# Linear attention: one scan per unit, one GpSimd chain for the scales, high parts of gated values on ScalarE a unit later

## The reference, cut to what matters

```python
q = layernorm(silu(causal_dwconv(h @ Wq)))         # 4 taps; the same for k
v, beta, gate = h @ Wv, sigmoid(h @ Wb + bb), silu(h @ Wg)
def step(S, inp):                                  # over the tokens
    S = (1.0 - b) * S + b * (v_t[..., :, None] * k_t[..., None, :])
    return S, einsum('bhvk,bhk->bhv', S, q_t)
out = (o * gate) @ Wo
```

## Time and profile before

| | |
|---|---|
| device time, three runs | 1381.65, 1390.52, 1396.57 us; median 1390.52 |
| profiled execution | span 1388.4 us from first to last instruction; its own time is not listed apart from the span |
| busy share of the span | PE 90%, DVE 75%, ACT 51%, POOL 48% |
| mean granted TensorE clock | 0.958 of full speed |
| linear attention | first convolution tap 410.0 us, last addition to `x_tok` 1329.2 us |

### The profile page before, as it was taken

One profiled execution on the slowest core, in us unless ns is written; L12 is line 12 of the kernel. 1 busy time (PEld: TensorE's weight loads), 2 busy tenths in 40 slices (PEclk: granted clock), 3 DMA queues, 4 the chain that ended last, 5 costly groups with the idle time before them and its releaser, 6 DMA issues. The chain is left out here.

```text
span 1388.4 us, 23212 instructions
## 1 busy us (share of the span) xinstructions
PE 1247.3 (90%) x7062; PEld 959.6 (69%) x7062; DVE 1036.7 (75%) x2130; ACT 711.5 (51%) x1336; POOL 670.5 (48%) x1678
## 2 busy tenths in 40 slices
PE   4899999996978889998999998998999999899769
PEld 3455545445747778777877787877877787788646
DVE  6747676746337888888888888888888788788652
ACT  2236555572436464655555555646555555546323
POOL 6000000001606766666666766666666766676620
PEclk9569999998999999999999999999999999999989
DMA  6414333303020111001001101011000100010010
GB/s 150 52 31 56 54 48 47 47 2 105 2 80 25 35 54 35 24 24 64 32 25 54 34 23 65 23 34 54 34 23 23 64 29 28 24 34 12 1 61 1
DMA packets 25098, 56.00 MB, mean 40 GB/s; under 512 B 3831, under 2 KB 8823, under 8 KB 23863
## 3 DMA queue, kind: packets, MB, share of 16 engines
q1 hardware_dynamic: 25015, 55.11, 15.7%
HBM read 39.95 MB, written 2.29 MB: 30 GB/s over the span
## 5 line engine op out<-in xcount | busy, mean ns | idle before, releaser
L1483 DVE SCALAR_TENSOR_TENSOR l_conv<-l_proj_k,par,l_conv 128x511 f32<-128x511 f32 (+2 forms) x192 | 142.6, 743 | 114.0 <-ACT l_conv L1401 113.9
L536 DVE TENSOR_REDUCE a_neg_max<-a_scores 128x1 f32<-128x512 f32 x236 | 157.2, 687 | 78.4 <-PE a_scores L342 77.9
L1401 ACT ACTIVATE l_conv<-l_proj_q,par 128x512 f32<-128x512 f32 x64 | 44.1, 689 | 263.3 <-PE l_proj_q L1271 263.3
L479 ACT ACTIVATE a_probs<-a_scores_t 128x1024 f32<-128x1024 f32 x128 | 125.6, 1021 | 73.7 <-PE a_scores_t L357 73.3
L1483 DVE SCALAR_TENSOR_TENSOR l_conv<-l_proj_q,par,l_conv 128x511 f32<-128x511 f32 (+2 forms) x192 | 143.1, 745 | 24.9 <-ACT l_conv L1401 18.3
L1492 DVE TENSOR_TENSOR_SCAN l_decay<-l_keep,l_diag 128x256 f32<-128x256 f32 (+1 forms) x256 | 157.0, 652 | 0.1
L1418 ACT ACTIVATE l_normed<-l_turn_q,l_shift,l_scale 128x128 f32<-128x128 f32 x256 | 96.2, 457 | 96.5 <-POOL l_shift L1218 96.3
L85 POOL MEMSET ln_minus_half_b<- 128x4 f32 x1 | 0.1, 101 | 299.3 <-POOLq L592 299.3
L1215 POOL TENSOR_TENSOR l_scale<-l_small,l_minus_half 128x4 f32<-128x4 f32 x128 | 130.1, 1016 | 10.0
L1359 PE MATMUL l_outp<-l_masked,l_values 128*128 128x128 f32 (+1 forms) x512 | 111.3, 342 | 0.9 <-DVE x_tok L1570 0.9
L342 PE MATMUL a_scores<-a_k_stack,a_q_stack 48*128 48x512 f32 x236 | 109.5, 476 | 2.8 <-DMA a_k_stack<-a_dense_lo 1.7
(11 more groups left out here) (292 smaller groups left out, 3655.9 us busy)
## 6 DMA issues: line engine op xcount, KB each, us to landing
l_keep<-keep_rows SPq DMA_DIRECT2D x64, 384.0 KB, 3.4
head_raw<-w_heads SPq DMA_DIRECT2D x8, 1024.0 KB, 4.9
a_q_stack<-a_dense_hi SPq DMA_DIRECT2D x32, 128.0 KB, 4.2
a_k_stack<-a_dense_hi SPq DMA_DIRECT2D x32, 128.0 KB, 5.0
x_tok<-x SPq DMA_DIRECT2D x4, 512.0 KB, 6.4
a_q_stack<-a_dense_lo SPq DMA_DIRECT2D x16, 128.0 KB, 3.8
a_k_stack<-a_dense_lo SPq DMA_DIRECT2D x16, 128.0 KB, 5.3
wo_raw<-w_o SPq DMA_DIRECT2D x1, 2048.0 KB, 11.1
```

The costliest lines, as they stand in the source:

```text
L479: act.activation(probs[:, n % 2, 2 * half:2 * half + 2, :], scores_t[half][:], ACT.Exp, scale=SOFT_SCALE).then_inc(probs_done, 1)
L536: dve.tensor_reduce(neg_max[:, g % 2, j:j + 1], max_bank(g, j), AX.X, ALU.max, negate=True).then_inc(max_done, 1)
L1483: ins = dve.scalar_tensor_tensor(conv[:, w, m, s:], proj[w][:, 0:SEQ - s], par[:, h, tap:tap + 1], conv[:, w, m, s:], ALU.mult, ALU.add)
```

## The change

Three things change in `linear_attention`, and the stage before it prepares for one of them.

- **One scan.** The `keep` row of a unit gets the order of the tiles as they lie in `decay` (256, 256, 128, 128 columns), with a zero at the start of each, and `diag` the matching identities; one scan of 768 columns takes the place of four. It stands behind tap q2 and in front of tap k1. `norm_and_decay` writes the second halves once more and sets the zeros: per sequence one more DVE instruction of 16x256 and two memsets, a semaphore wait between. A row holds 1024 numbers in place of 768, as does its load.
- **One chain.** POOL waits for the statistics of q and of k, and runs the ten small instructions once, on eight columns; ACT's norm of q and of k wait for its end.
- **High parts.** `gated_hi` of unit u - 4 is a copy on ACT, first in its step; `gated_low` of u - 4 stands on POOL behind the scales and in front of `decayed`.

```diff
 HALF = SEQ // 2
+CAUSAL = SEQ + HALF
+KEEP = CAUSAL + HALF
 def f32(ap):
...
                 dve.tensor_scalar(keep[:, b, 0:SEQ], beta_rows[:, b, :], -1.0, 1.0, ALU.mult, ALU.add).then_inc(kept, 1)
-                dve.wait_ge(kept, i + 1)
+                second = beta_rows[:, b, :].rearrange("p (h t s) -> p h t s", h=2, t=2)[:, :, 1, :]
+                dve.tensor_scalar(keep[:, b, SEQ:CAUSAL].rearrange("p (h s) -> p h s", h=2), second, -1.0, 1.0,
+                                  ALU.mult, ALU.add).then_inc(kept, 1)
+                dve.wait_ge(kept, 2 * (i + 1))
                 if i == 0:
                     dve.wait_ge(zeros_set, 1)
-                dve.tensor_tensor_scan(keep[:, b, SEQ:], keep[:, b, HALF:SEQ], zeros[:], 1.0, ALU.mult,
-                                       ALU.add).then_inc(keep_done, 1)
+                dve.tensor_tensor_scan(keep[:, b, CAUSAL:], keep[:, b, HALF:SEQ], zeros[:], 1.0, ALU.mult,
+                                       ALU.add).then_inc(multiplied, 1)
+                dve.wait_ge(multiplied, i + 1)
+                for w, at in ((HALF, 0), (P, SEQ)):
+                    starts = keep[:, b, at:at + 2 * w].rearrange("p (h s) -> p h s", h=2)[:, :, 0:1]
+                    dve.memset(starts, 0.0).then_inc(keep_done, 1)
             dve.wait_ge(turned_done, NB)
...
         quarter = sb("quarter", [P, 2 * TPB])
-        diag = sb("diag", [P, SEQ])
-        keep = sb("keep", [P, 4, SEQ + HALF])
+        diag = sb("diag", [P, CAUSAL])
+        keep = sb("keep", [P, 4, KEEP])
         conv = sb("conv", [P, 2, 2, SEQ])
...
                 row = keep_rows[bass.ds(2 * pair + e, 1), b, :]
-                sp.dma_start(keep[:, k % 4, :], row.to_broadcast([P, SEQ + HALF])).then_inc(keep_loaded[k % 4], 16)
+                sp.dma_start(keep[:, k % 4, :], row.to_broadcast([P, KEEP])).then_inc(keep_loaded[k % 4], 16)
                 if k == 1 and not (isinstance(pair, int) and pair + 1 >= PAIRS):
...
             pool.memset(quarter[:], 0.25).then_inc(consts_set, 1)
-            pool.memset(diag[:, P:], 0.0).then_inc(consts_set, 1)
-            pool.tensor_copy(diag[:, 0:P], ident[:]).then_inc(consts_set, 1)
-            def scales(v, k, w):
-                i, tiles = k % 2, slice(w * TPB, (w + 1) * TPB)
-                st = stats[:, i, tiles]
-                wait(pool, stats_done[w], v + 1)
-                wait(pool, norm_done[w], v - 1)
+            wide_diag = diag[:, 0:SEQ].rearrange("p (h s) -> p h s", h=2)
+            pool.memset(wide_diag[:, :, P:], 0.0).then_inc(consts_set, 1)
+            pool.tensor_copy(wide_diag[:, :, 0:P], ident[:].unsqueeze(1).to_broadcast([P, 2, P])).then_inc(consts_set, 1)
+            pool.tensor_copy(diag[:, SEQ:].rearrange("p (h s) -> p h s", h=2),
+                             ident[:].unsqueeze(1).to_broadcast([P, 2, P])).then_inc(consts_set, 1)
+            def scales(v, k):
+                i, tiles = k % 2, slice(0, 2 * TPB)
+                st = stats[:, i]
+                for w in range(2):
+                    wait(pool, stats_done[w], v + 1)
+                    wait(pool, norm_done[w], v - 1)
                 pool.tensor_tensor(small[:, 1, tiles], st[:, :, 1], st[:, :, 4], ALU.subtract)
-                pool.tensor_tensor(small[:, 2, tiles], st[:, :, 2], st[:, :, 5], ALU.add).then_inc(stat_step[w], 1)
+                pool.tensor_tensor(small[:, 2, tiles], st[:, :, 2], st[:, :, 5], ALU.add).then_inc(stat_step, 1)
                 pool.tensor_tensor(small[:, 0, tiles], st[:, :, 1], st[:, :, 4], ALU.add)
...
-                wait(pool, stat_step[w], 4 * v + 4)
+                                   ALU.add).then_inc(stat_step, 1)
+                wait(pool, stat_step, 4 * v + 4)
                 pool.tensor_tensor(scale[:, i, tiles], small[:, 7, tiles], minus_half[:, tiles],
-                                   ALU.pow).then_inc(scales_ready[w], 1)
-                wait(pool, scales_ready[w], 2 * v + 1)
+                                   ALU.pow).then_inc(scales_ready, 1)
+                wait(pool, scales_ready, 2 * v + 1)
                 pool.tensor_tensor(shift[:, i, tiles], small[:, 5, tiles], scale[:, i, tiles],
-                                   ALU.mult).then_inc(scales_ready[w], 1)
+                                   ALU.mult).then_inc(scales_ready, 1)
             def decayed(v, k, rows_in):
...
                 wait(pool, read_out, v - 3)
-                pool.tensor_tensor(q_late[:, r, :], qk[:, 0, m, HALF:], keep[:, r, SEQ:],
+                pool.tensor_tensor(q_late[:, r, :], qk[:, 0, m, HALF:], keep[:, r, CAUSAL:],
                                    ALU.mult).then_inc(q_decayed, 1)
...
                                    ALU.subtract).then_inc(gated_lo_done, 1)
-            pool.wait_ge(consts_set, 4)
+            pool.wait_ge(consts_set, 5)
             def step(pair, k, u):
                 if has(u, 1):
-                    for w in range(2):
-                        scales(u - 1, (k - 1) % BODY, w)
+                    scales(u - 1, (k - 1) % BODY)
+                if has(u, 4):
+                    gated_low(u - 4, (k - 4) % BODY)
+                if has(u, 1):
                     decayed(u - 1, (k - 1) % BODY, keep_count(pair, k))
-                if has(u, 3):
-                    gated_low(u - 3, (k - 3) % BODY)
-            steps(pool, step, 3)
+            steps(pool, step, 4)
         @block.tensor
...
                 m = k % 2
-                wait(act, scales_ready[w], 2 * v + 2)
+                wait(act, scales_ready, 2 * v + 2)
                 wait(act, returned[w], v)
...
                 last.then_inc(norm_done[w], 1)
+            def gated_high(v, k):
+                wait(act, gated_done, v + 1)
+                wait(act, out_done, v - 2 - k % 2)
+                act.activation(gated_hi[:, k % 4, :], gated[:, k % 2, :], ACT.Copy).then_inc(gated_hi_done, 1)
             def high_weights(u, part):
...
                 new_weights = k == BODY - 1 and not (isinstance(pair, int) and pair + 1 >= PAIRS)
+                if has(u, 4):
+                    gated_high(u - 4, (k - 4) % BODY)
                 if has(u, 0):
...
                 return dve.tensor_tensor(masked[:, k % 2, at:at + n], score[:, 0:n], decay[:, at:at + n], ALU.mult)
-            def scan(r, tiles):
-                for i in tiles:
-                    last = dve.tensor_tensor_scan(decay[:, START[i]:START[i] + WIDTH[i]], keep[:, r, i * P:i * P + WIDTH[i]],
-                                                  diag[:, 0:WIDTH[i]], 0.0, ALU.mult, ALU.add)
-                return last
             def low_weights(pair, part):
...
                         wait(dve, turned[w], v + 1)
-                        wait(dve, scales_ready[w], 2 * (v - 1))
+                        wait(dve, scales_ready, 2 * (v - 1))
                         for t in range(TPB):
...
                     convolve(pair, k, u, 0, 2)
-                    convolve(pair, k, u, 1, 1)
-                    convolve(pair, k, u, 0, 3)
-                    convolve(pair, k, u, 1, 2)
                 if has(u, 1):
                     wait(dve, k_decayed, v)
-                    scan(kk % 4, [0])
+                    dve.tensor_tensor_scan(decay[:], keep[:, kk % 4, 0:CAUSAL], diag[:], 0.0, ALU.mult,
+                                           ALU.add).then_inc(decay_done, 1)
+                if has(u, 0):
+                    convolve(pair, k, u, 1, 1)
+                    convolve(pair, k, u, 0, 3)
+                    convolve(pair, k, u, 1, 2)
                 if has(u, 3):
...
                     convolve(pair, k, u, 1, 3)
-                if has(u, 3):
-                    v, r = u - 3, (k - 3) % 4
-                    wait(dve, gated_done, v + 1)
-                    wait(dve, out_done, v - 2 - (k - 3) % 2)
-                    dve.tensor_scalar(gated_hi[:, r, :], gated[:, r % 2, :], 1.0, 0.0, ALU.mult,
-                                      ALU.add).then_inc(gated_hi_done, 1)
                 if k == BODY - 1 and not (isinstance(pair, int) and pair + 1 >= PAIRS):
                     low_weights(pair + 1, Q)
-                if has(u, 1):
-                    scan((k - 1) % 4, [1, 2, 3]).then_inc(decay_done, 1)
                 if has(u, 0):
```

More of the change, by code:

```diff
@@ L937, in norm_and_decay @@
         beta_rows = sb("beta_rows", [LH, NB, SEQ])
-        keep = sb("keep", [LH, NB, SEQ + HALF])
+        keep = sb("keep", [LH, NB, KEEP])
         zeros = sb("zeros", [LH, HALF])
@@ L1210, in scales @@
                 pool.tensor_scalar(small[:, 5, tiles], small[:, 0, tiles], -0.5, 0.0, ALU.mult, ALU.add)
[L1211 removed]
+                wait(pool, stat_step, 4 * v + 3)
                 pool.tensor_tensor(small[:, 7, tiles], small[:, 6, tiles], small[:, 4, tiles],
[L1213 to L1214 removed]
+                                   ALU.add).then_inc(stat_step, 1)
+                wait(pool, stat_step, 4 * v + 4)
@@ L1469, in step @@
                         high_weights(u, part)
```

(2 more changed lines are left out.)

29 lines of the change are left out of this document (13 added, 16 removed).

## The result

The change made the kernel slower: 1398.65 us (median of 19 runs, 1396.83 to 1411.16) against 1383.16 us (19 runs, 1380.48 to 1397.33) for the kernel before on the same chips. The ratio is 1.0102, with a 95% interval of 1.0077 to 1.0127. The prediction said 1361 us and gave "slower" a chance of 0.10.

A forecast was written before the change was run, and what follows sets the result against it. DVE's work and POOL's chain in series were taken to bound the 13.76 us unit. Savings of 26.5 (ordinary units) and 4 (changes of pair), less 0.7, gave span 1358.6, or 1361 us; forecast range 1350 to 1372, whole 1333 to 1386.

The forecast's parts named there:

- What leaves the ring: DVE between tap k1 and the statistics: scans and high parts leave, 3.26 us in all per unit.
- the new scan: DVE's scan of 768 columns: 1.75 us, mostly hidden in the 1.93 us that DVE waited for tap k.
- high parts on ACT: ACT ahead of first tap q: at most 0.76 us, covered by 4.19 us of idle time, so no cost.
- The one chain: POOL's ten small instructions on eight columns: only the power grows, by 0.61, making the chain 3.62 us.
- the rival that it costs the same: POOL's power costs the same on eight columns as on four: 1337 us; chance 0.14.
- Ring 1: Loop from addition through statistics, POOL's chain, norm of q and PE's output projection: closes the unit at 13.26 us.
- Of 64 units some 53 are ordinary: Linear attention's units: 0.50 us saved in each of 53, 26.5 us together.
- Changes of pair: Seven units where DVE makes low parts of weights: 0.6 us saved each, 4 us; bounds 0 and 1.2 each.
- Stage before, +0.7: `norm_and_decay`'s extra instruction, memsets and wait: mostly hidden by idle time, 0.7 us more; bounds 0.3 and 1.5.
- The scan gets in ahead of the chain's end: DVE's scan ready before POOL's last small instruction, which then waits: unit 14.9 us, 1452 us; chance 0.10.
- Next to nothing: POOL's power doubles to 2.07, or the lock delays gating by 0.6 us each unit: 1386 us; chance 0.16.
- the second rival: DVE's scan starts before POOL's last small instruction, adding 1.2 x 53 = 62 us: 1452 us; chance 0.10.

The follow-up runs named there:

- e4: Changed kernel with POOL's power on four columns, keys' scales left at 1.0 (16 added empty instructions appear in no trace): 1348.88 us, ratio 0.976 to the kernel before.
- e13: Changed kernel, DVE's loop head at slot 0, low parts of head weights on 16 of 512 columns from the second pair: 1359.23 us, ratio 0.9791.
- e6: Changed kernel with the head of DVE's loop set at slot 0, removing its fetch stall: 1378.71 us, ratio 0.9977 to the kernel before.
- e8: Kernel before with a hint for the jump back at the head of GpSimd's loop: 1374.44 us, ratio 0.9944 to the unedited kernel before.
- e5: Changed kernel with a hint for the jump back at the head of DVE's loop: 1379.61 us, ratio 0.9991 to the kernel before.
- e9: Changed kernel with two POOL chains restored (queries, then keys) and the heads of DVE's and GpSimd's loops at slot 0: 1314.94 us, ratio 0.9501.
- e12: Changed kernel with only the two POOL chains restored, no loop placed: 1330.57 us, ratio 0.9612 to the kernel before.
- e11: Changed kernel with two chains, both loop heads at slot 0, and scan and values' low parts later at a change of pair: 1345.69 us, ratio 0.972.
- e7: Kernel before with the head of DVE's loop set at slot 200, giving DVE a fetch stall: 1387.84 us, ratio 1.0024 to the unedited kernel before.

## Why the prediction was wrong, step by step

- **What leaves the ring, the new scan, high parts on ACT: right.** DVE no longer waits ahead of k1, the scan takes 1.75 alone (856.68) and 2.55 behind `gated_low`, the high parts 0.62 on ACT under idle time that is still 3.55.
- **The one chain: right.** The power on eight columns took 1.64, as computed from the earlier trace rows; the rival that it costs the same is out. The worth of this step was confirmed by e4, and e4's unit of 12.86 is close to that rival's 12.82.
- **Ring 1: the right ring, 0.24 too short.** I took 0.08 from the earlier trace rows for POOL's start behind the statistics. There POOL had just ended `gated_low`, and 0.08 was its gap behind its own instruction; released by DVE's semaphore it starts after 0.23. The chain is 3.69 instead of 3.62. A ring that gains half a microsecond lost half its gain to this: 0.25 x 42 = 10.6 us.
- **"Of 64 units some 53 are ordinary": too many.** 42 distances are; the first seven grew by 1.5 together and the unit behind a change is no ordinary one: 11 x 0.5 + 1.5, some 7 us.
- **Changes of pair, "I take 0.6: 4 us": this step failed, and decided the sign.** They cost 22.9 us more. I saw that the low parts and the scan both hit the chain and then let four scans less weigh against it, without following the queue. 19.8 of it came with the fetch stall on DVE (17.8 at the jumps back themselves), for which my sum had no term. The kernel before has no such stall on DVE (0.31 to 0.35 at the branch) and one on GpSimd, to be seen as those 0.89 us of idle time at 849.31, which I didn't read. The other 3.1, and the 4 us not gained, are the chain held by low parts and scan, and the clock (e13, e6): with no stall on either side (e6 against e8) the changes themselves are 4.0 us longer where I had them 4 shorter, and the units behind them 7.7 longer, a term that the sum didn't have. With these four corrections (10.6, 7, 26.9, and the 0.7 left out) the forecast's -29.8 becomes the +14.0 of the distances. The sign that I had set for being wrong, an addition that doesn't wait for PE, looks at the ordinary unit alone and could not catch this.
- **Stage before, +0.7: not seen.** The first gate of linear attention starts anywhere from 405 to 419 us in these profiles, so 0.7 can't be read off.
- **The rivals.** "The scan gets in ahead of the chain's end" came true, but only at the changes of pair, where the low parts make the chain late enough; in the ordinary unit the scan starts 0.31 us behind the chain's end (914.66 against 914.35). "Next to nothing" is what e5 and e6 give, by another road. In the second rival 1.2 x 53 is 64 and not 62; nothing hangs on it. PE alone closes a unit in 12.68 (e9), where I had put 12.80.

I also never asked which part of the change was worth having. e9 and e12 answer: the single scan and the move of the high parts together bring the unit to PE's own 12.68 (no run has one without the other); joining the chains costs 0.82 of it and the room at a change of pair, since the queries then wait for the statistics and the power of the keys.

## What to carry to other kernels

Price the irregular units of a loop as closely as the regular ones, with the queue of each engine written down for them: seven of them outweighed 42 here. Work that is shared between an urgent and a patient consumer (scales of queries and keys) should not be joined for the sake of fewer instructions; the urgent one pays. And when the number of an engine's instructions changes ahead of or inside a hardware loop, look at the engine's first instruction behind each jump back for idle time that ends at nothing, or at an instruction long done (the 0.89 us here), and at the packets of the instruction queue: a stall can appear, or vanish, with no change to the work.

## What the runs showed of the hardware

- Between a jump back and the next record of its sequencer an engine needs 0.23 to 0.35 us or 2.5 to 3.7 us, and each long one comes with some 5 packets on the instruction queue. The hint or a loop head at slot 0 gave the short time at each jump back in the runs that had one (e5, e6, e8 to e11, e13). The entry into GpSimd's placed loop took 2.9 us (e9, e11). Which loops have the long time I can't derive. The places that an edit set are these: DVE's loop of 317 instructions is slow from slot 200 (e7), its loop of 277 fast from slot 0 (e6), GpSimd's of 295 fast from slot 0 (e9). Unplaced, the first is fast (0.31 to 0.35, before) and the other two slow (2.8 to 2.9, changed; 2.5 to 3.7, before), and GpSimd's loop of 215 is fast (0.27 to 0.31, changed); at which slots these four lie, the traces don't show.
- The stall costs what the queue lets through: 3.5 to 3.9 us per jump where 0.91 us of work was left to DVE at the branch, 0.2 where 3.11 was (e7).
- A power costs by its columns on GpSimd: 0.57, 1.03 and 1.64 us on one, four and eight, where the other small instructions stay at 0.20. A scan takes 0.39, 0.68 and 1.75 us on 128, 256 and 768 columns.
- Of a DVE instruction that reads from SBUF alone and one of POOL, the later was held in these places. The scan of 128 columns ended 0.28 us behind POOL's 1236 before; that of 768 took 2.55 instead of 1.75 behind `gated_low`, and a small instruction of 0.20 took 1.20 (changed), 1.33 (e6) and 1.55 (e9) beside it. The high parts before, with one input, take 0.42 at the least and 0.96 where they begin beside the decayed queries (914.65 + 0.74), and end 0.28 behind them. The addition to `x_tok`, with one input in PSUM, and `gated_low` keep their 0.68 and 1.28 side by side (904.18 and 904.38).
- After the same 3.25 us of idle time PE's clock fell at four changes of pair of e6 and not at one, to 0.50 for 3.4 us, which cost 1.6 to 1.7 us each time.
